# A picture layer on one core: the first picture loaded in two parts, the last four steps written out, and 24 products of zeros on TensorE in the first steps

## The reference

```python
gray  = sum(weight[c] * x[c])                     # three colours to one
edge  = (abs(conv3x3(gray, sx)) + abs(conv3x3(gray, sx.T))) / 2
h     = edge + time_mix(layernorm(edge))          # rows of the picture are tokens of 256
out   = h + experts(layernorm(h))                 # 8 experts, the best one by its logit
# time_mix: k, v, r = mixtures of a token with the one before it, times Wk, Wv, Wr;
#   a decaying running sum over the 256 tokens (wkv), gated by sigmoid(r), times Wo
# experts: gelu((xhat * scale + bias) @ W1 + b1) @ W2 + b2, kept where the expert is the token's best
```

## Time and profile before

| | us |
|---|---|
| median of three runs | 1120.14 |
| profiled execution, whole run | 1121.44 |
| profiled execution, span of the core (first to last instruction) | 1119.8 |
| PE busy | 1069.8 |
| DVE busy | 1024.5 |
| ACT busy | 989.4 |
| POOL busy | 283.0 |

### The profile page before, as it was taken

The page is one execution under the profiler, slowest core; times in us unless marked ns, Lnnn a source line. Parts: engine busy times, 40 slices in busy tenths (PEclk is TensorE's granted clock), DMA queues, the critical chain, the costliest instruction groups (busy, mean ns, idle before and its releaser), DMA issues.

```text
span 1119.8 us, 17777 instructions
## 1 busy us (share of the span) xinstructions
PE 1069.8 (96%) x6097; PEld 777.9 (69%) x6097; DVE 1024.5 (91%) x1867; ACT 989.4 (88%) x1581; POOL 283.0 (25%) x298
## 2 busy tenths in 40 slices
PE   7767999999999999999999999999999999999887
PEld 2344777777777777778777777777777777777665
DVE  4689999999999999999999999999999999999820
ACT  0569899999999999999999999999999999999642
POOL 3431123322212333322122332231223332210001
PEclk8889999999999999999999999999999999999989
DMA  9697878999889889999999899999999899771223
GB/s 172 148 177 152 161 108 159 168 179 188 171 150 163 162 158 175 174 189 171 152 162 169 161 158 181 182 173 156 161 166 163 157 179 181 125 120 27 37 38 38
DMA packets 177776, 168.31 MB, mean 150 GB/s; under 512 B 14352, under 2 KB 177742, under 8 KB 177742
## 3 DMA queue, kind: packets, MB, share of 16 engines
q1 hardware_dynamic: 126358, 118.50, 48.3%
q0 software_dynamic: 50048, 48.25, 34.0%
q10 hardware_dynamic: 1336, 1.12, 0.5%
HBM read 102.80 MB, written 80.76 MB: 164 GB/s over the span
## 4 chain that ended last, share of the span: by engine, by line
PE 87%; ACT 5%; DVE 3%; SPq 2%; issue 1%; POOL 1%; DMA 0%; POOLq 0%; DVEq 0%; ACTq 0%
PE bank L1628 24%; PE bank L1803 20%; PE bank L1742 15%; PE bank L1727 10%; PE bank L1666 9%; PE bank L1637 5%; PE bank L1649 1%; PE bank L1804 1%; PE bank L1757 1%; PE bank L1767 1%; SPq L336 1%; ACT hidden L1278 1%; SPq L361 1%; DMA planes<-in_x_dram 0%; DVE gap L590 0%
## 5 line engine op out<-in xcount | busy, mean ns | idle before, releaser
L1803 PE MATMUL bank<-w_sb,hidden 128*128 128x256 f32 x1024 | 240.8, 382 | 3.7 <-ACT hidden L1278 3.6
L475 POOL DMA_DIRECT2D out_dram<-moe x64 | 76.3, 1192 | 619.7 <-ACT moe L1290 600.2
L1803 PEld LDWEIGHTS bank<-w_sb,hidden 128*128 128x128 f32 x1024 | 185.6, 191 | 33.2 <-ACT hidden L1278 5.2
L1727 PE MATMUL bank<-w_o_t,den 128*128 128x256 f32 x512 | 120.8, 390 | 4.1 <-DVE den L663 4.1
L1666 PE MATMUL bank<-rows_in,conv_w 102*32 102x512 f32 x960 | 110.3, 599 | 0.0
L1742 PE MATMUL bank<-normed_hi,w_hi 128*128 128x512 f32 x256 | 110.0, 430 | 0.0
L1727 PEld LDWEIGHTS bank<-w_o_t,den 128*128 128x128 f32 x512 | 97.0, 194 | 17.7 <-DVE den L663 5.3
L1742 PE MATMUL bank<-normed_lo,w_hi 128*128 128x512 f32 x256 | 101.0, 394 | 0.0
L1742 PE MATMUL bank<-normed_hi,w_lo 128*128 128x512 f32 x256 | 100.9, 394 | 0.0
L605 DVE TENSOR_TENSOR_SCAN max_state<-neg_exp_w,bank 128x256 f32<-128x256 f32 x128 | 80.7, 672 | 12.3 <-PE bank L1628 12.3
L590 DVE SCALAR_TENSOR_TENSOR mixed_vr<-normed,params,normed_t 128x512 f32<-128x512 f32 x128 | 91.3, 755 | 0.0
(11 more groups left out here) (166 smaller groups left out, 2679.1 us busy)
## 6 DMA issues: line engine op xcount, KB each, us to landing
rows_in<-gray_dram SPq DMA_DIRECT2D x180, 256.0 KB
planes<-in_x_dram SPq DMA_DIRECT2D x120, 256.0 KB, 8.1
gray_dram<-planes POOLq DMA_DIRECT2D x120, 256.0 KB, 5.8
out_dram<-resid SPq DMA_DIRECT2D x64, 256.0 KB, 4.7
out_dram<-moe POOLq DMA_DIRECT2D x64, 256.0 KB, 5.3
gray_dram<-in_x_dram SPq DMA_DIRECT2D x60, 256.0 KB, 4.9
rows_in<-gray_dram SPq DMA_DIRECT2D x120, 24.0 KB
rows_in<-in_x_dram SPq DMA_DIRECT2D x9, 256.0 KB
```

The source lines that it names most:

```text
L475: pool.dma_start(out_rows(at.j, at.u - FFN, half), moe[:, 2 * half:2 * half + 2, :], accum_op=ALU.add).then_inc(added[half], 16)
L1727: ins = pe.matmul(bank[BANK_WO[half]][:, i * D:(i + 1) * D], rwkv[:, 2 * kt + i, half * P:(half + 1) * P], w_t[3][:, kt, :], start=(kt == ...
L1803: pe.matmul(ps, hidden[:, m, i, rows], w2_sb[:, m, :], start=(m == 0), stop=False)
```

## The change

The first pictures: each of the two pictures of pair 0 is loaded in two halves of four row tiles, with ten DMAs instead of five; the upper halves count on a semaphore of their own (`s_top_rows`), and PE convolves the upper halves (convolutions 1 and 0) before it waits for the lower. SP waits for the whole first pair before it issues Wk, Wv, Wr (now all three on SP), W1 and what follows. `scharr_dj` is no longer loaded but copied on DVE out of `scharr_all`, in nine small instructions ahead of `color_w`; b2 is issued by ACT, behind a wait for POOL's clearing; the outer rows of the second buffer are cleared after `color_w`; six multiplies of `color_w` become three of twice the width.

The split of Wk, Wv, Wr leaves POOL: ACT writes the high part from PSUM (`high_weights`) and DVE subtracts it from PSUM (`low_weights`).

PE has a new function `keep_busy`, which multiplies zeros into a PSUM bank that is free. It is called at six places of `first_steps`, with 6, 3, 2, 6, 5 and 2 products, 24 in all; WARM_UP falls from 7 to 4. The orders of `first_steps` on PE, DVE and ACT change in many places.

`run_steps` ends after step 32 (LAST_STEPS = 1) on PE, DVE and ACT, and steps 33 to 36 are `last_steps`, a hand-written order like `first_steps`. SP and POOL keep their loops. `step`, and with it steps 6 to 32, does not change. The diff, cut to its core:

```diff
-WARM_UP = 7
+WARM_UP = 4
+LAST_STEPS = 1
...
+        def load_first_colors(eng, i):
+            base = i * NCOL * T * D
+            for half, loaded in ((0, s_top_rows), (1, rows_loaded[0])):
+                tile = half * TILES // 2
+                for color in range(NCOL):
+                    src = bass.AP(x.tensor, base + color * T * D + tile * ROW_TILE * D,
+                                  [[D, ROW_TILE], [ROW_TILE * D, TILES // 2], [1, D]])
+                    eng.dma_start(rows_in[0][ROW_TILE * color:ROW_TILE * (color + 1), tile:tile + TILES // 2, i, :], src
+                                  ).then_inc(loaded, 16)
...
-            load_colors(sp, 0, 0)
-            for src, dst in zip((Wk, Wv), w_raw):
+            load_first_colors(sp, 0)
+            sp.wait_ge(rows_loaded[0], 16 * X_DMAS)
+            for src, dst in zip((Wk, Wv, Wr), w_raw):
                 sp.dma_start(dst, src.rearrange("(a p) c -> p a c", p=P)).then_inc(s_w_in, 16)
-            for dj in range(3):
-                sp.dma_start(scharr_dj[ROW_TILE * dj:ROW_TILE * (dj + 1), :],
...
-            pool.wait_ge(s_act_setup, 5)
-            split_weights(0)
-            split_weights(1)
-            split_weights(2)
...
+            for dj in range(3):
+                ins = dve.tensor_scalar(scharr_dj[ROW_TILE * dj:ROW_TILE * (dj + 1), :],
+                                        scharr_all[ROW_TILE * dj:ROW_TILE * (dj + 1), dj:18:3],
+                                        0.5 * GRAY_WEIGHTS[2], None, ALU.mult)
+            for n in range(6):
+                rows, dj = slice(3 * ROW_TILE, TAPS - n), 2 - n % 3
+                dve.tensor_scalar(scharr_dj[rows, :], scharr_all[rows, dj:18:3], 0.5 * GRAY_WEIGHTS[2], None,
+                                  ALU.mult).then_inc(s_edges_w, 1)
+                dve.wait_ge(s_edges_w, n + 1)
...
+            def low_weights(i):
+                done(dve.tensor_tensor(w_lo[i][:, :, :].rearrange("p a d -> p (a d)"), bank[BANK_W[i]][:, :],
+                                       w_hi[i][:, :, :].rearrange("p a d -> p (a d)").bitcast(F32), ALU.subtract))
...
+            def high_weights(i):
+                act.activation(w_hi[i][:, :, :].rearrange("p a d -> p (a d)"), bank[BANK_W[i]][:, :], ACT.Copy
+                               ).then_inc(s_act_setup, 1)
...
+            def keep_busy(ps, products):
+                for _ in range(products):
+                    pe.matmul(ps[:, 0:D], zeros[:, 0:P], zeros[:, 0:D], start=True, stop=True)
...
@@ PE, first_steps @@
+                pe.wait_ge(s_top_rows, 160)
+                convolve(1, EDGE, pair(0, EDGE), waits=False)
+                convolve(0, EDGE, pair(0, EDGE), waits=False)
                 pe.wait_ge(rows_loaded[0], 160)
                 convolve(3, EDGE, pair(0, EDGE), waits=False)
                 convolve(2, EDGE, pair(0, EDGE), waits=False)
...
+                pe.wait_ge(s_abs[0], 1)
+                keep_busy(bank[BANK_NORMED[1]], 6)
                 pe.wait_ge(s_normed, 1)
...
+                pe.wait_ge(s_dve_setup, 19)
+                project_v(1, WKV, pair(0, WKV), waits=False)
                 pe.wait_ge(s_low_k, 1)
-                pe.wait_ge(s_pool_setup, 2)
                 project_k(1, WKV, pair(0, WKV), waits=False)
                 pe.wait_ge(s_abs[0], 2)
                 project_k(0, EDGE, pair(0, EDGE), waits=False)
+                pe.wait_ge(s_gap[0], 1)
+                keep_busy(bank[BANK_NORMED[1]], 3)
+                pe.wait_ge(s_normed, 2)
...
+                pe.wait_ge(s_abs[2], 2)
+                keep_busy(bank[BANK_R[1]], 2)
...
+                pe.wait_ge(s_gap[1], 1)
+                keep_busy(bank[BANK_K[1]], 6)
+                pe.wait_ge(s_low_k, 2)
...
+                pe.wait_ge(s_v[1], 1)
+                keep_busy(bank[BANK_EDGE[3]], 5)
                 pe.wait_ge(rows_loaded[0], 320)
...
+                pe.wait_ge(s_gate[0], 2)
+                keep_busy(bank[BANK_NORMED2[0]], 2)
+                pe.wait_ge(s_normed2, 1)
...
@@ ACT, first_steps @@
-                scaled(0, GRAY, pair(2, GRAY), waits=False)
-                act.wait_ge(s_normed_ps[1], 1)
-                copy_normed(1, EDGE, pair(0, EDGE), waits=False)
                 act.wait_ge(s_normed_ps[0], 1)
                 copy_normed(0, EDGE, pair(0, EDGE), waits=False)
...
+                act.wait_ge(s_edge_ps[0], 2)
+                absolute(0, EDGE, pair(1, EDGE), waits=False)
+                scaled(0, GRAY, pair(2, GRAY), waits=False)
+                scaled(1, GRAY, pair(2, GRAY), waits=False)
...
-            run_steps(pe, step, first=FIRST_STEPS)
+            run_steps(pe, step, first=FIRST_STEPS, last=LAST_STEPS)
+            def last_steps():
...
+                pe.wait_ge(s_normed2_lo[0], 30)
+                project_v(0, EDGE, pair(31, EDGE), waits=False)
+                pe.wait_ge(s_logits_t, 30)
+                transpose_logits(PROJ, pair(29, PROJ), waits=False)
+                project_v(1, WKV, pair(31, WKV), waits=False)
+                pe.wait_ge(s_hits, 30)
+                project_k(1, WKV, pair(31, WKV), waits=False)
+                project_k(0, EDGE, pair(31, EDGE), waits=False)
+                first_layer(2, FFN, pair(29, FFN), waits=False)
+                pe.wait_ge(s_result[1], 29)
+                pe.wait_ge(s_rwkv, 31)
+                output_projection(1, PROJ, pair(30, PROJ), waits=False)
+                output_projection(0, PROJ, pair(30, PROJ), waits=False)
...
@@ ACT, last_steps @@
...
+                act.wait_ge(s_r_ps[1], 32)
+                gate_of(1, WKV, pair(31, WKV), waits=False)
+                gate_of(0, WKV, pair(31, WKV), waits=False)
+                act.wait_ge(s_den, 32)
+                act.preload_act_table_set("natural_log_exp_and_others")
+                log_denominator(PROJ, pair(31, PROJ), waits=False)
+                act.wait_ge(s_normed2_ps[1], 31)
+                copy_normed2_high(1, PROJ, pair(30, PROJ), waits=False)
+                act.wait_ge(s_log_den, 32)
+                reciprocal(PROJ, pair(31, PROJ), waits=False)
```

More of the change, by code:

```diff
@@ L278, in load_colors @@
                               ).then_inc(rows_loaded[buf], 16)
+        def load_first_colors(eng, i):
[7 more added lines that the diff above has]
+                                  ).then_inc(loaded, 16)
+                if half == 0:
+                    eng.wait_ge(s_outside, 2)
+                for k in range(2):
+                    start, end = max(tile, 1 - k), min(tile + TILES // 2, TILES - k)
+                    src = bass.AP(x.tensor, base + (start * ROW_TILE + (ROW_TILE if k else -1)) * D,
+                                  [[T * D, NCOL], [ROW_TILE * D, end - start], [1, D]])
+                    first = 3 * ROW_TILE + 3 * k
+                    eng.dma_start(rows_in[0][first:first + 3, start:end, i, :], src).then_inc(loaded, 16)
         def load_rows(eng, buf, i):
@@ L308, in pair, with run_steps @@
             return Step((p + stage) // UNROLL, (p + stage) % UNROLL, PAIRS)
-        def run_steps(eng, step, first=0, before={}):
+        def run_steps(eng, step, first=0, last=FFN, before={}):
             for n in range(first, 2 * UNROLL):
@@ L318, in run_steps @@
                     step(Step(j, i, PAIRS))
-            for i in range(FFN):
+            for i in range(last):
                 step(Step(PAIRS // UNROLL, i, PAIRS))
@@ L545, in _ @@
             assert own[0] == SETUP_FIRST
-            dve.wait_ge(s_scharr_dj_in, 80)
-            done(dve.tensor_scalar(scharr_dj[0:TAPS, :], scharr_dj[0:TAPS, :], 0.5 * GRAY_WEIGHTS[2], None, ALU.mult))
+            for b in range(1, 2):
+                clear_outside(b)
             for di in range(3):
@@ L932, in first_steps @@
                 aggregate(0, EDGE, pair(1, EDGE), waits=False)
+                low_weights(2)
+                dve.wait_ge(s_rstd[0], 2)
+                shift(0, EDGE, pair(1, EDGE), waits=False)
+                dve.wait_ge(s_k_ps[0], 1)
+                running_max(0, EDGE, pair(0, EDGE), waits=False)
+                dve.wait_ge(s_max[0], 1)
+                gap_of(0, EDGE, pair(0, EDGE), waits=False)
+                running_max(1, EDGE, pair(0, EDGE), waits=False)
+                dve.wait_ge(s_max[1], 1)
@@ L961, in first_steps @@
-                running_max(0, EDGE, pair(1, EDGE), waits=False)
-                dve.wait_ge(s_k_ps[1], 2)
-                running_max(1, EDGE, pair(1, EDGE), waits=False)
+                gap_of(1, EDGE, pair(1, EDGE), waits=False)
                 dve.wait_ge(s_gate[1], 1)
@@ L966, in first_steps @@
                 gate_numerator(WKV, pair(0, WKV), waits=False)
-                dve.wait_ge(s_max[0], 2)
-                gap_of(0, EDGE, pair(1, EDGE), waits=False)
-                dve.wait_ge(s_max[1], 2)
-                gap_of(1, EDGE, pair(1, EDGE), waits=False)
+                mix_r(EDGE, pair(1, EDGE), waits=False)
                 dve.wait_ge(s_recip, 1)
@@ new lines, in first_steps @@
```

(22 more changed lines are left out.)

890 lines of the change are left out of this document (603 added, 287 removed).

## The result

Four runs of the changed kernel took 1102.7, 1103.89, 1103.93 and 1105.61 us: a median of 1103.91, against 1121.04 of the four runs of the kernel before that it is compared with. The ratio is 0.9849, its 95% interval 0.9837 to 0.9860. The profiled execution has a span of 1102.2 us, 17.6 less than before. The forecast of 1102 is 1.9 us off and the range holds the time, but the sum's two terms were both off by some 3 us, in opposite directions.

The account below looks back on a forecast made before the run. The prediction took PE, busy 1069.8 of 1119.8 us, as the bound, with idle and lower-clock time to win in start and end. Span 1119.8 - 8 (start) - 10 (end) = 1101.8, median about 1102 us, range 1093 to 1112.

Parts of the forecast that it names:

- First convolution: Start, PE's first convolution of pair 0: begins at 11.5 us instead of 16.53, -5.0 us.
- `low_k`: Start, DVE, pair 0: ends at about 41.4 us instead of 51.79, -10.4 us.
- The way to the first `gated_wkv`: Start, pair 0: `den_scan` at about 59.3 us, -5, then `gated_wkv` about 10 to 11 us earlier.
- The second `gated_wkv`: Start, pair 1: at about 107.4 us instead of 117.56, about 10 to 11 us earlier.
- step 6: End of the start: step 6 begins at 139.7 us instead of 147.75, -8 us.
- Rival A: Start: pair 2 comes late through scaling, POOL's additions and row loads; start gives -3, 1107 us; chance 0.15.
- The products: Start, PE: 24 products, 10.4 us, counted at nothing except 3 behind `gap`, up to 2.3 us.
- Rival B: Start and end: products of zeros keep the clock up; start -13, end -11.6, 1095 us; chance 0.16.
- The end: Last steps: earlier projections and `gated_wkv`, one stretch left at the lower clock; -10 us, between -3.5 and -12.
- D: From step 6: DVE owed work, so that step runs longer and the start's gain is lost; 1110 us; chance 0.08.
- C: Start, PE: all 24 products lie on the path, 20.8 us at the lower clock; +2.8, 1123 us; chance 0.04.
- E: Products don't hold the clock, lower-clock stretches come at new places; start -4, end -9, 1107 us; chance 0.07.

Follow-up runs that it names:

- e4: The changed kernel with the nine small DVE instructions that build `scharr_dj` moved behind `color_w`: 1104.10 us.
- e3: The changed kernel with ACT's scaling of pair 3's planes moved earlier, to the gap at 42.75 us: 1101.66 us.
- e5: The changed kernel with both moves, ACT's scaling of pair 3's planes earlier and the nine small DVE instructions behind `color_w`: 1099.58 us.
- e2: The changed kernel without the 24 products of `keep_busy`: 1107.52 us.
- e7: The kernel before with only the new last four steps, its start the old one: 1108.48 us.
- e11: e5 with 18 more products of zeros at four waits behind which its trace showed the lower clock: 1094.66 us.
- e1: The changed kernel with its new start, but steps 32 to 36 through `step` as in the kernel before: 1116.28 us.
- e8: The changed kernel with 16 more products of zeros before PE's wait for pair 3's rows: 1104.13 us.

## Why the prediction was right, and where it was not

The direction was right. That the total was too is luck: two misses nearly cancel, +3.5 us in the start and -3.1 in the end.

**First convolution, -5.0 forecast, -4.3 found (12.22).** `color_w` held it, as said. The term that was mis-sized is the nine small instructions: 1.5 us by nine times 0.17, measured 3.8 (4.79 to 8.55). I took the duration of one lone instruction for that of all nine. The first three, which don't wait for each other, took 0.28, 1.17 and 0.16; the six that each wait for the one before took 0.50 and 0.18 in turn. Why they differ is not shown. The table was there 0.9 us earlier and the wider multiplies saved 0.9, which made up for some of it. e4 then shows that this error cost nothing in the change as it is.

**`low_k`, -10.4 forecast, -9.5 found** (ends at 42.30). The contention with POOL went as costed: mixtures at 1.41 us, `low_k` at 1.23.

**The way to the first `gated_wkv`: -10 to -11 forecast, -14.1 found.** `den_scan` came at 56.78, not 59.3; the three products behind the gap cost 1.56 of the 2.3 us allowed.

**The second `gated_wkv`: -10 to -11 forecast, -5.9 found; step 6: -8 forecast, -4.5 found.** This is the step that failed: PE's wait for pair 3's rows, 7.1 us, is not in the sum, which has 1.5 us for all the waits of the new order. I followed pair 2's rows and found them in time, which they nearly were (a wait of 1.1 us), and didn't follow pair 3's. Even pair 2's time was luck: I took over the 28 us from scaling to loads, of which POOL's split of the weights was a part (its turn came at 50.79, behind the split). Without the split it was 17 us (40.07 to 56.98), and the loads then took until 69.9. Rival A had the mechanism, ACT's scaling, POOL's additions and SP's loads as a chain that doesn't get shorter when the rest does, but on the wrong pair. In the kernel before SP issued pair 3's rows at 82.76 us, in the change at 81.33: 1.4 us earlier, while everything around them came 6 to 14 us earlier. The chain's head even moved back, ACT's scaling from 54.12 to 59.02, by the new order itself; I followed `scaled` of pair 2 on ACT and not that of pair 3. e3 and e5, which move it forward, lose the wait. The 11.85 us of the red addition stood beside SP's loads of pair 2's rows and of the next planes; that these slowed it is argued from the timeline, not shown by a run.

**The products: counted at nothing, found to be 3 us (e2), in that trace the whole gain of the start.** I asked what they cost, 10.4 us behind 26.0 of waiting, and that was right: no more than 2.6 us of them stood on the path. I didn't ask what the new order would do without them; by e2 against e7 it would have given 1.0 us, where I had 8. Rival B, the clock that stays up, gave 1095, and had 0.16; the change reached a clock of 0.92 in the start. e11 comes to rival B's number, with 0.99 and 1094.7, but not by the products alone: the two moves are in it, and the 18 more products are 4.9 of its 9.3 us.

**The end: -10 forecast, -13.1 found, beyond the bound of -12.** The steps in it were right: the projection of pair 30 takes 3.61 us instead of 5.41, and `gated_wkv` of pair 31 starts 51.5 us after the first convolution of step 33 (1006.15) where it started 62.7 after it (1010.65 to 1073.31), 11.2 earlier where I had 9.5. The rows of PE and DVE after the change:

```profile
1039.48 3.61 PE L2025 MATMUL bank<-w_o_t,den 128*128 128x256 f32 x16
...
1057.66 1.23 DVE L671 TENSOR_TENSOR den<-bonus,den 128x1024 f32<-128x1024 f32 x1 [0.62 <-ACT den L1339]
```

The last product of the first layer ends 17.1 us earlier against the span's start (1104.60 to 1087.48), 12.6 by the mark of step 33. Two terms were mis-sized: the stretch at the lower clock that I left in, +1.7, didn't come (1.00), and the 15.2 us behind the last product became 14.7. The rest, about 1 us, is in the order itself. The bound of -12 was set too tight: the idle time and the clock of the earlier trace rows allow 13.6. The profile before was also one with much of the lower clock in its end: against that of e1 the same new end gained only 8.4.

**Two slips in the sums.** A second `gated_wkv` at 107.4 and a way to step 6 that is not shorter give 137.6 and not 138.2, and 1104.60 less 1092.7 is 11.9 and not 11.6. Neither changes the reading.

**Rivals.** D (DVE owed work at step 6): no, the middle is 861.31 us. C (all the products on the path): no, 2.6 us of them. E (they don't hold the clock): no, 0.92 against 0.83 without them (e2).

## What to carry to other kernels

When a chain of work is made shorter, follow each stream of transfers that feeds it, pair by pair, until one is found that doesn't move: here the pictures of pairs 0 to 2 came earlier and those of pair 3 didn't, and the gain ended there. Look at where the new order puts the work at the head of each stream: ACT's scaling of pair 3 had moved 5 us back. A shortened chain makes new gaps, and a gap can cost the clock of what follows, so gaps have to be filled in the same edit; the filling showed its worth only where the wait behind it wasn't the bound (e8 nothing, e11 4.9 us over e5). For a row of small instructions take the time of such a row from a trace, not the duration of one times their number.

## What the hardware showed

Products of zeros hold TensorE's granted clock: with 16 of them in the 7.1 us before the convolution of pair 3 it took 2.78 us instead of 4.66 (e8), and with 42 in the start the clock there is 0.99 (e11, whose two moves shorten waits as well), with none 0.83 (e2). Where they ended too early they did not: in the change 6 of them ended at 58.1 us, PE stood for 2.15 and the clock fell (0.70 from 60.25 to 66); in e11, with 10 there, PE stood for 0.28 and it kept 1.00. The Trainium skill ("TensorE: Matmul & The Clock Gate", Part 1) has the lower level as the default and activity as what releases it; the runs agree, and add that the operands may be zeros.

The same old end took 109.15 us in one profiled execution and 104.4 in another, with clocks of 0.95 and 1.00 and nearly the same idle time (8.8 and 9.4 us). An accumulating DMA that takes 5.8 us as a rule took 11.85 when four plane loads and ten row loads were issued beside it.
